# Value products of an attention head in two lots of sixteen instead of four lots of eight

## What is computed

```python
content_score = jnp.einsum('bthd,bshd->bhts', q + u_bias, k)
pos_score = _rel_shift(jnp.einsum('bthd,phd->bhtp', q + v_bias, p))
attn = jax.nn.softmax((content_score + pos_score) / math.sqrt(dh), axis=-1)
ctx = jnp.einsum('bhts,bshd->bthd', attn, v).reshape(b, t, d)
return ctx @ Wout.T + bout
```

## Time and profile before

| | us |
|---|---|
| median of 3 runs | 1256.58 |
| lowest and highest | 1253.76 and 1261.54 |
| the profiled execution | 1258.67 |
| its span in the profile | 1256.9 |

### The profile page before, as it was taken

How to read it: one execution, slowest core, us unless ns; L and a number is a source line. 1 busy time by engine, 2 the same in 40 slices (tenths; PEclk the granted TensorE clock), 3 DMA queues, 4 the chain that set the end, 5 groups by cost and what they waited for, 6 DMA issues and landing times.

```text
span 1256.9 us, 22649 instructions
## 1 busy us (share of the span) xinstructions
PE 905.8 (72%) x8587; PEld 668.4 (53%) x8587; DVE 808.6 (64%) x1632; ACT 464.3 (37%) x745; POOL 328.4 (26%) x361
## 2 busy tenths in 40 slices
PE   0149587999899999953379999999936880257674
PEld 0123476888788788743235655655523770145453
DVE  1735353554455455412768888888886868989885
ACT  0365032333333333322845555555544123111211
POOL 6552000233233323355800000000036035211211
PEclk9769798999999999986679999999977995587876
DMA  9005511332233233211300000000000000000000
GB/s 120 0 19 140 178 36 26 72 77 60 66 71 67 60 71 77 52 46 23 100 1 2 1 0 0 0 0 0 0 15 0 1 1 17 1 0 17 17 17 17
DMA packets 68829, 46.10 MB, mean 37 GB/s; under 512 B 34489, under 2 KB 60065, under 8 KB 68033
## 3 DMA queue, kind: packets, MB, share of 16 engines
q1 hardware_dynamic: 51600, 24.05, 9.6%
q0 software_dynamic: 8448, 19.81, 6.3%
q10 hardware_dynamic: 8704, 1.19, 0.6%
HBM read 30.05 MB, written 12.06 MB: 34 GB/s over the span
## 4 chain that ended last, share of the span: by engine, by line
PE 49%; DVE 18%; issue 9%; ACT 8%; DMA 6%; POOL 5%; ACTq 3%; SPq 1%; POOLq 0%; DVEq 0%
PE PS L801 7%; PE PS L876 5%; PE PS L878 5%; PE PS L877 5%; PE PS L821 4%; PE PS L781 4%; PE PS L782 4%; PE PS L805 3%; ACTq L598 3%; PE PS L753 3%; ACT HN L566 2%; DMA YC<-queries_content 2%; DVE STAT L1037 2%; DVE HB L1235 2%; PE PS L1012 1%
## 5 line engine op out<-in xcount | busy, mean ns | idle before, releaser
L1118 DVE TENSOR_REDUCE MX<-PS 128x2 f32<-128x512 f32 x256 | 170.8, 688 | 197.5 <-PE PS L782 196.0
L618 ACT ACTIVATE REG<-PS 128x1024 f32<-128x1024 f32 x128 | 131.3, 1026 | 254.1 <-PE PS L805 251.3
L801 PE MATMUL PS<-XP,TB 96*128 96x64 f16 x2048 | 159.7, 246 | 1.6 <-DMA XC<-NEG 1.6
L781 PE MATMUL PS<-TM,YP 128*128 128x256 f16 x512 | 129.6, 285 | 40.9 <-DMA YC<-queries_content 22.9
L801 PEld LDWEIGHTS PS<-XP,TB 96*128 96x128 f16 x2048 | 130.9, 120 | 29.3 <-issue 21.5
L782 PE MATMUL PS<-KM,YC 128*128 128x256 f16 x512 | 125.8, 278 | 0.0
L876 PE MATMUL PS<-XH,W 128*128 (+1 forms) x256 | 99.1, 387 | 24.6 <-DVE HB L1235 24.6
L661 ACT ACTIVATE SG<-PS 128x512 f32<-128x512 f32 x128 | 76.3, 597 | 106.0 <-PE PS L878 105.7
L1235 DVE SCALAR_TENSOR_TENSOR HB<-PS,SG 128x512 f32<-128x512 f32 x128 | 87.1, 686 | 35.3 <-ACT SG L661 33.1
L805 PE MATMUL PS<-XC,KC 97*128 97x128 f16 x1024 | 107.3, 228 | 0.0
L781 PEld LDWEIGHTS PS<-TM,YP 128*128 128x128 f16 x512 | 73.3, 143 | 49.9 <-DMA YC<-queries_content 25.3
(11 more groups left out here) (229 smaller groups left out, 1760.6 us busy)
## 6 DMA issues: line engine op xcount, KB each, us to landing
REG<-inverse_sums POOLq DMA_DIRECT2D x64, 128.0 KB, 3.1
YC<-queries_content ACTq DMA_DIRECT2D x224, 4.0 KB
KC<-keys_strips SPq DMA_DIRECT2D x16, 192.0 KB
keys_strips<-REG POOLq DMA_DIRECT2D x12, 224.0 KB, 8.0
R<-in_L_attn_x SPq DMA_DIRECT2D x8, 256.0 KB, 13.3
R<-REG POOLq DMA_DIRECT2D x64, 32.0 KB, 2.5
out<-R SPq DMA_DIRECT2D x64, 32.0 KB, 1.6
queries_position<-REG POOLq DMA_DIRECT2D x2, 960.0 KB, 8.7
```

The source lines that it names most:

```text
L618: A(P[jt][:, 1024 * up:1024 * up + 1024].rearrange("p (k x) -> p k x", k=2), ST[u % 2], ACT.Exp).then_inc(exp_done, 1)
L781: mm(o, yp[:, a], TM[p][:, 31 - a:31 - a + T], start=True, stop=False)
L801: mm(o_pos[:, a], TB[p][0:96, y0:y0 + 128], xp[0:96, 8 * bank + a], start=(a == 0), stop=False, skip_group_check=True)
L1118: nc.vector.tensor_reduce(MX[h % 2][:, 2 * kk:2 * kk + 2], banks[4 + kk % 2].rearrange("p (a j) -> p a j", a=2), AX_X, ALU.max)\
```

## The change

The two lots of keys jt = 1 of the head before are issued together, behind step 4, and the two lots of keys jt = 0 of the head itself together, behind step 12. The last two lots of all, behind the loop, stood together before and stay so. Nothing else changes.

```diff
@@ -831,10 +831,12 @@
                     if h + 1 < H and k < 12:
                         for kk in range(16 * k // 12, 16 * (k + 1) // 12):
                             maximum_scores(h + 1, kk)
-                    if h and k in (3, 6):
-                        context_part(h - 1, 1, int(k == 6))
-                    if k in (11, 14):
-                        context_part(h, 0, int(k == 14))
+                    if h and k == 4:
+                        context_part(h - 1, 1, 0)
+                        context_part(h - 1, 1, 1)
+                    if k == 12:
+                        context_part(h, 0, 0)
+                        context_part(h, 0, 1)
             context_part(H - 1, 1, 0)
             context_part(H - 1, 1, 1)
```

## The result

The changed kernel is slower: 1290.89 us (median of 6, 1287.18 to 1294.18) against 1257.78 us for the kernel before (6 runs beside it). The ratio is 1.0263, interval 1.0229 to 1.0297: 33 us lost where 4.5 were to be gained. Its profiled execution took 1294.18 us with a span of 1292.4.

A forecast was written before the change was run, and what follows sets the result against it. TensorE was taken to set the pace. Heads 1 to 13 save 13 x (0.24 + 0.17) = 5.3 us, head 0 loses 0.9, later merges are covered: 4.5 us off the median 1256.58 gives 1252.1 us, range 1246 to 1259.5.

The forecast's parts named there:

- What a merge saves: On TensorE, two lots of 1.10 us issued together become one of 1.96, saving 0.24 us; bounds 0 and 0.66.
- nothing is saved: Rival, chance 0.13: a merge in mid-stream saves nothing, so the kernel is 2.0 us slower, 1258.6 us.
- more is saved: Rival, chance 0.10: the change of mode costs more in mid-stream, a merge is worth 0.45 us, 1246.4 us.
- Step 12: Merge at step 12, heads 1 to 13: exponential 7, YC and the next head come 0.17 us earlier.
- The idle time in rows 3: TensorE's wait for YC's DMAs, once per head, 1.1 us in an ordinary head; claimed to stay about 1.2.
- Head 0: First head: its only merge delays exponential 6 and everything behind it, 0.86 us lost; wait ahead of head 1 7.9 us.
- The clock rival: Heads' starts, chance 0.07: TensorE's clock falls behind longer waits, 1.64 us a head, 1273.4 us if in all 13.
- the thinner end: End of a head: four steps follow one another without a lot, then the wait; could lower the clock, 1.64 us a head.
- The long wait in one head: One 2.47 us wait with a fall of the clock in the profiled execution, which other executions need not have.
- The cover behind head 14: Heads 14 and 15: four merges save nothing behind 515 us, as another chain ends 10 us after TensorE's last lot.

The follow-up runs named there:

- e3_u6_free: The changed kernel with no DMAs of YC behind exponential 6 and four behind exponential 5: 1251.92 us, ratio 0.9953.
- e1_sp_late: The changed kernel with SyncE's bulk for the next head waiting for one pair of scores more: 1249.61 us, ratio 0.9938.
- e4: The kernel before with only the lots of steps 3 and 6 merged behind step 4: 1252.01 us, ratio 0.9966.
- f2_step13: The changed kernel with the merged lots of step 12 put behind step 13 instead: 1248.22 us, ratio 0.9891.
- g2: The changed kernel with three redundant, already fulfilled waits in SyncE's queue ahead of its bulk: 1254.84 us in one run.
- f3_yc_early: As f2_step13, with the DMAs of YC behind exponentials 0 to 3 of a head, four each: 1225.78 us, ratio 0.9727.

## Why the prediction was wrong

- *What a merge saves* was right: 1.96 us for a double lot in mid-stream, 0.24 a merge, the same as behind the loop. With the collision taken away, e3_u6_free has heads of 23.6 us, two merges less than 24.1, and measured 1251.92 us where 1252.1 was forecast; that the two agree so closely is partly luck, as the interval of its ratio is nearly 7 us wide. The rivals "nothing is saved" and "more is saved" are both out.
- *Step 12* is the step that failed. Its first part was right: 1.42 us between exponentials 6 and 7, ScalarE's queue late by 0.07. The error is in "So u = 7, and with it YC and the next head, comes ... 0.17 us earlier": it took the time from the issue of a DMA to its landing as fixed at what the earlier trace rows show. From exponential 7 to TensorE's next maximum it is 1.8 us in an ordinary head while YC is issued level with SyncE's TB, and 3.2 to 3.9 in the changed kernel, where it is a tenth behind. "The idle time in rows 3 stays at about 1.2" failed with it: it is 38.6 / 13 = 3.0 us. SyncE's queue, which begins 0.01 to 0.02 us ahead of those very DMAs, was no part of the argument. What stood as a term of 0.07 us was worth 1.7 us a head and, in 11 heads more than before, a fall of the clock.
- *Head 0* was right in kind: its wait grew from 6.77 to 7.58, where 7.9 was forecast. In e1_sp_late, with SyncE's bulk later, it was 5.33, so the bulk seems to lengthen this wait too.
- *The clock rival* (0.07) names the place, the direction and the price: a longer wait carries heads over the point, each then pays 1.64 us (1.6 found). Its cause was taken as a slower issue or the thinner end; e1_sp_late, with the same thin end and full clock in 11 heads of 13, rules that out as a cause. It was the landing. The changed kernel's waits of 2.6 to 3.3 us lie above the 1.58 from which the clock was seen to fall. Its 1273 lacked the longer waits themselves, 22.5 us.
- *The long wait in one head* (2.47 us) was taken for an accident of that execution. It comes back at the same head in e1, e3, e4 and f2, with 2.6 to 2.8 us, and in g2 with 3.1, so it is part of the kernel. In e1 SyncE issues TB there 5.2 us behind YC, when TensorE has long gone on, and the wait is 2.76 us all the same, so it does not take SyncE's bulk to make it. Its cause stays open; in f3_yc_early it is gone with the others.
- *The cover behind head 14* was not tested by itself; the sum in which those four merges count for nothing held in e3_u6_free, but 1 us more or less could not be told there.

## What to carry to other kernels

A wait that the profile shows as "for a DMA" has two parts, issue and landing, and the second isn't a constant: before moving what stands ahead of a small, urgent DMA, read the other queues at the same microsecond, and see what bulk starts there. If an urgent transfer and a bulk transfer are released by the same event, give the urgent one a head start or move it away from the event; being level by luck is an edge, not a margin (in f2_step13 one level head besides the usual one waited 1.91 us). And when a reorder thins the work between two instructions of a queue, ask not only whether the queue still keeps up, but what else it was ahead of.

## What the runs showed of the hardware

- How long TensorE waited for two small DMAs turned on less than 0.1 us between two queues: issued 0.02 us before to 0.02 us after SyncE's TB, YC's two DMAs let TensorE go on after 1.1 to 1.5 us in nearly every head; issued 0.08 to 0.10 us after it, after 2.3 us or more in every head.
- A fulfilled wait in ScalarE's queue costs little but not nothing: three of them moved the next DMA issue from 0.01 to 0.08 us behind the start of the exponential.
- Behind waits of 1.1 to 1.5 us at the end of a head TensorE stayed at 2.4 GHz, and four thin steps ahead of them did not alter that. Behind one of 1.59 us in e1_sp_late it fell, and behind the waits of 2.6 to 3.3 us of the changed kernel it fell to 1.2 GHz in 12 heads of 13. The length of the wait alone does not settle it: there was no fall behind the one of 2.70 us in the changed kernel, nor behind one of 2.84 us in e3_u6_free.
